# Two preLN blocks on one core: the low half of the last FFN's input by VectorE from the bank, the last item's FFN by query tile, and new tables of slots, shifts and banks

## The reference, cut to what matters

```python
x = x + L0_attn(layernorm(x))   # logits - alpha[h] * |q - k|, softmax
x = x + L0_ffn(layernorm(x))    # three 128x128 products, tanh
x = x + L1_attn(layernorm(x))   # scores * exp(-0.01 |q - k|), softmax
x = x + L1_ffn(layernorm(x))    # 256->512->512->128, weights +1 or -1, relu between
# L1_ffn:
h = concatenate([x, -x]); h = relu(s0 * (h @ w0)) * 2
h = relu(s1 * (h @ w1)) * 2;  h = s2 * (h @ w2)
```

## Time and profile before

| what | value |
|---|---|
| median of 3 runs | 354.88 us (352.27 to 354.99) |
| the profiled execution | 355.89 us |
| its span on the core | 354.0 us |
| mean granted clock of TensorE over the span | 0.984 |

### The profile page before, as it was taken

One profiled execution on the slowest core, in us unless ns is written; L12 is line 12 of the kernel. 1 busy time (PEld: TensorE's weight loads), 2 busy tenths in 40 slices (PEclk: granted clock), 3 DMA queues, 4 the chain that ended last, 5 costly groups with the idle time before them and its releaser, 6 DMA issues.

```text
span 354.0 us, 11138 instructions
## 1 busy us (share of the span) xinstructions
PE 332.3 (94%) x3526; PEld 245.2 (69%) x3526; DVE 279.5 (79%) x1349; ACT 272.8 (77%) x588; POOL 260.6 (74%) x662
## 2 busy tenths in 40 slices
PE   6599979999999999999999989999999999999886
PEld 4266657777777777776767667777777777776664
DVE  6876789888989898888897968788587786866255
ACT  4576767877777777777878889898888889888832
POOL 6468767777777767777888898988888796868210
PEclk9879999999999999999999999999999999999989
DMA  5202642323233222324232324122241322011000
GB/s 140 67 1 66 163 131 77 108 74 113 72 115 119 67 89 95 100 88 119 80 106 73 116 70 113 34 85 84 80 120 33 107 62 79 3 49 34 0 17 30
DMA packets 42374, 28.14 MB, mean 79 GB/s; under 512 B 9095, under 2 KB 38478, under 8 KB 42318
## 3 DMA queue, kind: packets, MB, share of 16 engines
q1 hardware_dynamic: 41752, 27.18, 25.9%
q10 hardware_dynamic: 566, 0.26, 0.3%
HBM read 14.09 MB, written 13.09 MB: 77 GB/s over the span
## 4 chain that ended last, share of the span: by engine, by line
PE 73%; DVE 8%; ACT 5%; SPq 4%; DMA 4%; issue 4%; POOL 1%; POOLq 0%; DVEq 0%; ACTq 0%
PE bank L550 19%; PE bank L565 14%; PE bank L547 8%; PE bank L591 8%; PE bank L525 5%; PE bank L539 5%; PE bank L612 5%; PE bank L604 3%; SPq L1411 3%; DVE att_t L922 2%; PE bank L573 2%; DVE scored L857 2%; PE bank L657 2%; DMA dqk<-parts 1%; ACT probs L1078 1%
## 5 line engine op out<-in xcount | busy, mean ns | idle before, releaser
L1078 ACT ACTIVATE probs<-bank 128x512 f32<-128x512 f32 x256 | 148.4, 602 | 44.6 <-PE bank L550 39.2
L857 DVE CUSTOM_DVE_ANT_0 scored<-bank,decay 128x256 f32<-128x256 f32 x256 | 93.1, 415 | 25.0 <-PE bank L525 24.7
L1324 POOL TENSOR_SCALAR scored<-scored,negbias 128x256 f32<-128x256 f32 x224 | 105.9, 486 | 4.8
L857 DVE CUSTOM_DVE_ANT_0 scored<-bank,adist 128x256 f32<-128x256 f32 x256 | 92.6, 415 | 18.3 <-PE bank L525 15.1
L550 PE MATMUL bank<-ident,scored 128*128 128x128 f32 x704 | 103.5, 277 | 2.2 <-ACT probs L1078 1.8
L550 PEld LDWEIGHTS bank<-ident,scored 128*128 128x128 f32 x704 | 78.1, 141 | 26.0 <-issue 18.0
L565 PE MATMUL bank<-probs,vpad 128*32 128x256 f32 x1024 | 68.5, 385 | 0.0
L547 PE MATMUL bank<-ident,scored 128*128 128x128 f32 x320 | 48.5, 274 | 0.0
L1315 POOL TENSOR_SCALAR negbias<-mx 128x2 f32<-128x2 f32 x144 | 33.1, 237 | 18.0 <-DVE mx L857 17.4
L565 PEld LDWEIGHTS bank<-probs,vpad 128*32 128x32 f32 x1024 | 26.7, 109 | 25.1 <-issue 7.2
L857 DVE DVE_READ_ACCUMULATOR2_ANT mx<- 128x1 f32 x512 | 41.9, 82 | 0.0
(11 more groups left out here) (195 smaller groups left out, 447.2 us busy)
## 6 DMA issues: line engine op xcount, KB each, us to landing
dqk<-parts SPq DMA_DIRECT2D x120, 64.0 KB, 2.0
stack<-dqk SPq DMA_DIRECT2D x30, 256.0 KB, 2.9
dacc<-acc_sb SPq DMA_DIRECT2D x15, 256.0 KB, 2.2
att_rows<-dacc SPq DMA_DIRECT2D x15, 128.0 KB, 2.5
den_rows<-dden SPq DMA_DIRECT2D x15, 128.0 KB, 2.4
out_dram<-outb SPq DMA_DIRECT2D x8, 128.0 KB, 1.8
x_sb<-in_L_attn_x_dram SPq DMA_DIRECT2D x1, 640.0 KB, 4.5
den_in<-acc_sb SPq DMA_DIRECT2D x30, 8.0 KB
```

The source lines that it names most:

```text
L857: red = dve.tensor_tensor_reduce(scored[:, r, t, :], bank[c % QUAD][:, t * T:(t + 1) * T], tab[:, (1 - t) * P:(1 - t) * P + T], 1.0, NEG_B ...
L1078: act.activation(probs[:, c % RING, :, :], turn_bank(c)[:, :].rearrange("p (a c) -> p a c", a=2), ACT.Exp).then_inc(probs_ready, 1)
L1324: sh = pool.tensor_scalar(scored[:, r, t, :], scored[:, r, t, :], negbias[:, 2 * r + t:2 * r + t + 1], 1.0, ALU.add, ALU.mult)
```

## The change

It has four parts.

1. **The low half of the input.** In block 1 `act_ft` makes one copy, the float16 one. `low_input` runs on DVE, and reads the value from the bank itself in place of `fxn_t`. The bank is now free when DVE has done this (`f_lo`) and not when ACT has.
2. **The last item's FFN by query tile.** `h0` and `h1` of item 15 (and `h2`, `h3`) no longer are pairs of feature tiles but the two halves of the tokens, each with all 4 feature tiles; so t = 0 goes through both layers ahead of t = 1. The output has a bank for each half (`OUT_LAST`), an instruction of DVE for each (`dve_last_out`) and a DMA for each.
3. **The order of the end.** `att_t` of the last item is copied by DVE in place of ACT. PE projects item 15 before the output of item 13, does all of h2 of item 14 ahead of the transposed input of item 15, and one half of h3 ahead of `pe_last_in`. The low half of h1 of item 14 is POOL's and no longer DVE's.
4. **The tables.** Block 0 has 7 heads of kind P as before, 3 of D for 2 and 5 of G for 6. Block 1 has 2 of P for 3 and 9 of G for 8. Banks, slots, lags and the kinds that make the distance tables of iteration 0 are set anew.

```diff
-SHARED = ({"qk": 7, "v": 7, "ft": 0, "f0": 7, "proj": 7, "xn": 7},
-          {"qk": 1, "v": 0, "ft": 7, "f0": 7, "h3": 7, "h0": 0, "h1": 1,
-           "out": 0, "proj": 1, "xn": 0, "h2": 7})
+SHARED = ({"qk": 1, "v": 7, "ft": 7, "f0": 7, "proj": 7, "xn": 1},
+          {"qk": 1, "v": 7, "ft": 7, "f0": 7, "h3": 7, "h0": 0, "h1": 7,
+           "out": 1, "proj": 1, "xn": 0, "h2": 7})
...
-    "h0": (11, 9), "h1": (14, 9), "h2a": (15, 15), "h2b": (0, 0), "h3a": (0, 6), "h3b": (1, 7), "out": (0, 11),
+    "h0": (8, 9), "h1": (15, 11), "h2a": (15, 15), "h2b": (0, 0), "h3a": (1, 5), "h3b": (4, 7), "out": (0, 11),
...
-SHIFT = ("PPPG" "GGGD" "PDPP" "PGAG", "GPGD" "GGAP" "PGDA" "AGGG")
+SHIFT = ("PPGP" "DGGD" "GDPP" "PPGA", "GGGD" "GGAP" "PGDG" "AGAG")
...
-SHIFT_LAG = ("2121121123212311", "1321122223111112")
+SHIFT_LAG = ("3322212123212121", "1211122323112212")
...
-        last_reader[b] = (ft_sb, it + 1)
+        last_reader[b] = (f_lo, it - B + 1) if has1(it) else (ft_sb, it + 1)
...
+            if s == at("low_in", i) and has1(i - 2):
+                low_input(dve, i - 2)
...
-            act.activation(fx16[:, 0, :], ps[:, 0:T], ACT.Copy)
-        act.activation(fxn_t[:, :], ps[:, 0:T], ACT.Copy).then_inc(ft_sb, 1)
+            act.activation(fx16[:, 0, :], ps[:, 0:T], ACT.Copy).then_inc(ft_sb, 1)
...
-        eng.tensor_tensor(fx16[:, 1, :], fxn_t[:, :], fx16[:, 0, :], ALU.subtract).then_inc(f_lo, 1)
+        dve.tensor_tensor(fx16[:, 1, :], bank[bank_of("ft", f)][:, 0:T], fx16[:, 0, :], ALU.subtract).then_inc(f_lo, 1)
...
         pe_last_att_t(pe)
+        pe_proj(pe, c)
         pe_out(pe, a)
-        pe_proj(pe, c)
-        pe_hidden(pe, b, 2, [0])
+        pe_hidden(pe, b, 2, [0, 1])
         pe_ft(pe, c)
-        pe_hidden(pe, b, 2, [1])
+        pe_hidden(pe, b, 3, [0])
         pe_last_in(pe, 0)
         pe_last_in(pe, 1)
-        pe_hidden(pe, b, 3, [0, 1])
-        for half in range(2):
+        pe_hidden(pe, b, 3, [1])
+        for t in range(QT):
             for p in range(2):
-                for g in (2, 3):
-                    pe_last_deep(pe, g, half, p)
+                pe_last_deep(pe, t, p)
```

More of the change, by code:

```diff
@@ L740, in pe_last_in @@
             pe.wait_ge(f_lo, B)
-        for g in range(2):
-            for j in range(2):
-                k0 = (2 * g + j) * P
-                mm = pe.matmul(bank[bank_of(f"h{g}", LAST)][:, j * T:(j + 1) * T], w_ff0[:, k0:k0 + P], fx16[:, p, :],
-                               start=(p == 0 and j == 0), stop=(p == 1), skip_group_check=True)
+        for t in range(QT):
+            for k in range(4):
+                mm = pe.matmul(bank[bank_of(f"h{t}", LAST)][:, k * P:(k + 1) * P], w_ff0[:, k * P:(k + 1) * P],
+                               fx16[:, p, t * P:(t + 1) * P], start=(p == 0 and k == 0), stop=(p == 1),
+                               skip_group_check=True)
@@ L746, in pe_last_in, with pe_last_deep @@
             if p == 1:
                 mm.then_inc(last_h, 1)
[L749 to L753 removed]
+    def pe_last_deep(pe, t, p):
+        b = bank_of(f"h{2 + t}", LAST)
+        pe.wait_ge(last_lo if p else last_hi, t + 1)
+        if p == 0:
             bank_free(pe, b)
[L755 to L763 removed]
@@ L765, in pe_last_out @@
-    def pe_last_out(pe, half, p):
-        b = bank_of("out", LAST)
-        pe.wait_ge(last_lo if p else last_hi, half + 3)
-        if half == 0 and p == 0:
-            bank_free(pe, b)
-        for t in range(QT):
-            for k in (2 * half, 2 * half + 1):
-                mm = pe.matmul(bank[b][:, t * D:(t + 1) * D], fh_last[:, 1, p, k, t * P:(t + 1) * P], w_ff2[:, k, :],
-                               start=(half == 0 and p == 0 and t == 0 and k == 0),
-                               stop=(half == 1 and p == 1 and k == 3), skip_group_check=True)
-        if half == 1 and p == 1:
+        for n in range(4):
+            for k in range(4):
+                mm = pe.matmul(bank[b][:, n * P:(n + 1) * P], w_ff1[:, k, n * P:(n + 1) * P],
+                               fh_last[:, 0, p, k, t * P:(t + 1) * P], start=(p == 0 and n == 0 and k == 0),
+                               stop=(p == 1 and k == 3), skip_group_check=True)
@@ new lines, in pe_last_deep, with pe_last_out @@
+        if p == 1:
+            mm.then_inc(last_h, 1)
+            last_reader[b] = (last_sb, t + 3)
+    def pe_last_out(pe, t, p):
+        b = OUT_LAST[t]
+        pe.wait_ge(last_lo if p else last_hi, t + 3)
+        if p == 0:
+            bank_free(pe, b)
+        for k in range(4):
+            mm = pe.matmul(bank[b][:, 0:D], fh_last[:, 1, p, k, t * P:(t + 1) * P], w_ff2[:, k, :],
+                           start=(p == 0 and k == 0), stop=(p == 1 and k == 3), skip_group_check=True)
+        if p == 1:
@@ L1053, in dve_end @@
         dve_out(dve, b)
-        dve_out(dve, c)
+        for t in range(QT):
+            dve_last_out(dve, t)
     def act_hidden(act, it, g):
@@ L1381, in pool_iteration @@
                 low_qk(pool, i + 2)
-            if s == at("low_in", i) and has1(f):
-                low_input(pool, f)
             if s == at("low3", i) and has1(late):
```

88 lines of the change are left out of this document (41 added, 47 removed), and 12 rows, old and new, of tables (FIRST, SLOTS).

## The result

The changed kernel takes 349.01 us (median of 4 executions, 346.78 to 351.2) where the kernel before takes 354.39 (4 executions, 352.27 to 354.99): a ratio of 0.986, 95% interval 0.981 to 0.990. A second series of six gave 348.17 (346.21 to 351.39) beside 353.94, a ratio of 0.985 (0.981 to 0.989). The forecast was 348.0.

The account below looks back on a forecast made before the run. PE was taken as the bound, busy 94% of the span. Terms -0.6 - 0.4 - 3.4 + 0 - 2.9 = -7.3 gave execution 348.6, median 347.6; forecast 348.0 us, range 345.5 to 353.

Parts of the forecast that it names:

- The projection in items 10 to 15: Block 1: DVE's multiplication into att_t starts before POOL's low half of h1; with one P less, 6 x -0.57 = -3.4 us.
- the first rival: POOL starts its low half of h1 first, so DVE's multiplication into att_t waits again: 351.4 us; chance 25%.
- Items 8 and 9: First two items of block 1: one head of kind P less takes 0.22 off PE in each, -0.4 us.
- Block 0: Items 2 to 7: moving the layernorm statistics removes a 0.2 us stall per item, against a third D; -0.6 us.
- The end: Parts 2 and 3 at the program's end: five terms summing to -2.97, taken as -2.9 us.
- (a): End: projection of item 15 ahead of item 13's output starts residual, statistics and fxn earlier; -0.2 us.
- (b): End: POOL makes h1's low half, cutting PE's 2.20 us idle; if the clock stays up, 16 matmuls cost less; -1.6 us.
- (c): End: eight matmuls of h2 move into a gap ahead of the transposes of fxn; -0.87 us.
- (d): End, by query tile: the first half's evictions and low halves run beside PE's second half; -0.9 us.
- (e): End: first high half needed before any deep matmul of t = 0, with h3 covering 8 matmuls, not 16; +0.6 us.
- that rival: DVE becomes the bound through its added subtraction and low_input, making items longer: 358 to 361, 359.5 us; chance 6%.
- The start: Program start: PE's waits hang on an unchanged chain through DRAM; 0 us, with ends of -0.5 and +1.5.

Follow-up runs that it names:

- Experiment 2: Kernel before, with DVE's multiplication into att_t in block 1 moved one head earlier, to slot 13; ratio 0.9957.
- Experiment 3: Changed kernel, with ACT evicting h1 in block 1 in slot 11 instead of 12, so POOL starts first; ratio 0.9945.
- experiment 4: Changed kernel, with head 1 of block 1 of kind P again, as before; ratio 0.9866.
- the second profile: Changed kernel run and profiled again without any edit; ratio 0.985.
- experiments 8 and 9: Old tables and low_input: first with the new end order plus last FFN by query tile, then the order alone; ratios 0.9940 and 0.9951.
- experiment 7: Changed kernel with part 1 undone: in block 1 ACT copies the FFN input twice, POOL makes its low half; ratio 0.985.

## Why the prediction held, and where its terms were off

**The time.** 348.0 forecast, 349.01 and 348.17 measured, a gain of 5.4 and 5.8 on the medians where 6.9 was forecast. On the profiled pair it was 9.0 for 7.3. That the medians lie so near is in part luck: the term of items 10 to 15 was 1.4 too small, and the executions lost more than that in other places: items 8 and 9, block 0, and likely the start.

**The projection in items 10 to 15** is the step that carried the sum, and it went as written: POOL was placed 0.1 behind DVE and was 0.11 to 0.12 behind in items 11 to 15; L918 takes 0.42. Experiment 2 shows the wait was POOL's. Experiment 3 shows that the first rival's price was too low: 0.79 to 0.87 lost in each of five items where 0.57 was reckoned in six, 4.3 us in the stretch for 3.4 (352.96 measured for 351.4). So the margin of 0.1 decided more than the forecast had on it. The size was too small: 0.57 per item forecast, 0.68 to 1.01 found. The term was sized by item 12 alone. By experiment 2 the wait was worth 0.47 in items 11 and 12, but 0.62 to 0.69 in 13 to 15. The P is worth 0.17 to 0.19 in items 11 to 15 and not 0.22. Over items 10 to 15 the wait is 3.05 (experiment 2) and the P 1.34 (experiment 4), 4.4 of the 4.79.

**Items 8 and 9** is the step that failed: "in 8 and 9 alone 2 x -0.22" took a saving of PE for a saving of time. They got 0.13 longer (0.63 in the second profile); the 0.13 by itself is within the spread of the pair, the missing -0.4 is not: no profile with the new tables is below 35.77, the two shortest with the old ones are at 35.67 and 35.68. In these two PE isn't the bound all the time. A turn of item 9 in the profile after, timeline of PE, waits for POOL's subtraction:

```profile
184.30 0.66 PE L550 MATMUL bank<-ident,scored 128*128 128x128 f32 x4
185.47 1.09 PE L550 MATMUL bank<-ident,scored 128*128 128x128 f32 x8 [0.51 <-POOL scored L1322]
```

It starts 1.17 behind the turn ahead of it, where four transposes take 0.44 without a wait. Experiment 4 showed that the exchange of P for G isn't the cause; which of the lags and banks it is wasn't found.

**Block 0.** -0.42 for -0.6, but by another account: the stall went as said (item 2 to 4 at 17.34 for 17.50), the third D cost nothing in five of six items, and the loss sits in item 5, where DVE's weight conversions and a wait of L918 for POOL stand in the way, rows that the prediction had not looked at. With them spread, items 2 to 7 are 1.2 below the profile of before. But that one has a long item 7: against the three others with its block 0 (105.20 to 105.29) it is 0.9 to 1.0, and the seven profiles with the changed block 0 and no edit in it lie from 104.58 to 105.26, so 0 to 0.7 below these three. The -0.42 of the pair is one draw of many.

**The end.** -2.99 for -2.9. (a) -0.48 for -0.2, since POOL's `pow`, no longer beside DVE's subtraction, gained 0.3 too. (b) 16 matmuls at 0.11 for 0.21: -1.59, as forecast. (c) -0.87, as forecast: eight matmuls less behind the transposes, reckoned at the same spacing. (d) is the mis-sized term: -0.29 for -0.9; the deep layer and the output got 0.53 shorter up to the last matmuls, and from these to the end of the span, where the output now leaves in two stores, it takes 0.24 more, which I had taken at nothing. (e) 0.31 for 0.6. The five give -2.92 of the 2.99. What (d) gave too little, 0.61, (a) and (e) made up, so the sum was right by luck where its terms were not. For the query tiles themselves experiments 8 and 9 have 0.39, where (d) and (e) together forecast 0.3.

**Part 1** at nothing: right, 0.25 us in all by experiment 7. DVE didn't become the bound: it is busy for 80% of the span. (The sum of that rival, 348.0 + 4.2 + 6, gives 358.2; no term of it leads to 359.5 or 361.)

**The start** at 0 with a range to +1.5 can't be read from the pair of profiles. Item 2 begins at 55.2 to 56.4 in the four profiles with the old tables and at 54.9 to 59.4 in the seven with the new ones, on the mean 1.1 later, and all three at 0.50 or 0.57 are among the latter. Whether the new tables make the fall of the clock likelier wasn't tested. The executions without a profile point the same way: of the ten of the changed kernel the two with a mean clock of 0.995 took 346.2 and 346.8, those at 0.985 and 0.976 took 351.4 and 351.2. This is the likely reason why the medians show 5.4 and 5.8 and the profiles 9.0; it is not shown, since these executions have no trace.

## What to carry to other kernels

Where two engines can block each other for a whole instruction, look up both start times: 0.1 to 0.2 us of order decided 0.8 to 0.9 us of an item here, and moving the victim by one slot in the old kernel took the wait out with nothing else changed. Size a wait that is to go by each item in which it stands, not by one, and count a saving on the bounding engine only in the items where it bounds. Look at the start before comparing two profiles: what differs there may be the clock, or a transfer. Take the spread of an item from all profiles that have the same instructions before giving a difference a cause: item 5 and items 8 and 9 moved by 0.5 us here with no edit.
